# Six of seven sums of the heads' expert weights as three accumulating DMAs, with ten weight slots and new orders

## The chip, the cores and the metric

The kernel runs on one core of one Trainium2 chip. The metric is the device time of the whole program in microseconds (us). A core has five engines that run beside each other, each with its own instruction queue, in order: TensorE (PE), VectorE (DVE), ScalarE (ACT), GpSimd (POOL) and SyncE (SP), which here only issues DMAs.

## The reference

One layer of a perceiver-like model on x (64 batches x 64 rows x 128) and a context (64 x 128 x 96): cross attention with 16 heads, a tree attention with 16 heads, and a feed-forward part with product keys. The change lies in the last part:

```python
s1 = einsum('bshd,nd->bshn', q1, K1); s2 = einsum('bshd,nd->bshn', q2, K2)   # 8 heads, 32 keys each
v1, i1 = top_k(s1, 10);  v2, i2 = top_k(s2, 10)
vals, best = top_k(v1[..., :, None] + v2[..., None, :], 10)                 # 10 of the 1024 experts per head
scores = softmax(vals)
h = gelu(einsum('bsd,bshkd->bshk', x, W_down[expert_idx])) * scores
out = einsum('bshk,bshkd->bsd', h, W_up[expert_idx])
```

## The kernel before

The 4096 rows are 32 tiles of 128 rows (two batches a tile). No expert is gathered. For each head the kernel makes a dense row of 1024 weights: `e.s{h}` (PE) writes the 1024 sums of key scores to PSUM, `e.x{h}` (ACT) takes their exponent into `ew`, and `e.w{h}` (DVE, L1012) keeps those at or above the head's cut and writes zero elsewhere into a slot of `mw`, 128 x 1024 f32. POOL adds the eight heads' rows up into `wsum` in seven sums `e.a1` to `e.a7` (L1120). `e.wturn` (PE) transposes the sum, `e.gate` (DVE) multiplies it with the GELU of x times W_down (`e.hid` on PE, `e.gelu` on ACT with a table load before and after), `e.out` (PE) multiplies with W_up, and `e.add` (DVE) adds it to the residual `x3` and gives `y`, which `st.y` (SP) stores.

`mw` has NMW = 4 slots; head h uses slot h % 4. `e.w{h}` waits until the sum that read the slot is done.

The other steps that matter: `x.q0` to `x.q3` (PE, queries), copied out by `x.w0` to `x.w3`; `x.s0` to `x.s3` (PE, L377, scores, reading `cT`, which `ld.ct` loads); `x.x` (DVE, maxima), `x.e` (ACT, exponents, L705), `x.r` (DVE), `x.n` (POOL, L1071), `x.p` (PE, transposes), `x.t` (ACT), `y.m` (PE, mix with the context), `y.u` (ACT), `y.out` (PE, L439), `y.res` (DVE, L906, adds and takes statistics). Then the tree attention: `t.root` (POOL, L1058), `t.norm` (ACT, L686), `t.turn` (PE, L452), `t.sb`, `t.pv` (PE), `t.path` (DVE), `t.feat` (POOL), `t.fturn` (PE, L475), `t.fsb`, `t.sim`, `t.exp`, `t.mix`, `t.div`, `t.cturn`, `t.csb` (ACT, `actxT`), `t.out` (PE, L519), `t.res` (DVE). Then the keys: `k.root`, `k.norm`, `k.turn`, `k.high`, `k.low`, `k.key` (PE, L537 and L312 to L314, 512 columns), `k.top` (DVE), `k.split` (DVE), `k.kturn` (SP, a transposing DMA from `us` to `usT`, read by `e.s{h}`), `k.shift` (ACT, L766), `k.inner` (POOL), `k.cand` (DVE), `k.eb`, `k.z`, `k.lnz`.

The order on each engine is written out by hand in the five tables `PE_ORDER` to `SP_ORDER`: iteration i runs the steps from left to right, each for tile i minus its lag. Each step has its own semaphore; a step waits for its sources, for the readers of its destination, and for the step that last used its PSUM bank (table `BANK`).

Of the kernel before, what the change touches and what calls it, by code (L numbers as in the profile page):

```python
# [29 lines left out]
def build(nc, a):  # L30
# [3 lines left out]
    with ctx:  # L34
# [229 lines left out]
        def _(pe):  # L264
# [96 lines left out]
            def scores(k):  # L361
                def step(t):
                    if k == 0:
                        pe.wait_ge(s["x.w0"], t + 1)
                    elif k == 1:
                        pe.wait_ge(s["x.w3"], t + 1)
                    elif k == 2:
                        pe.wait_ge(s["x.w1"], t + 1)
                    elif k == 3:
                        pe.wait_ge(s["x.e0"], t + 1)  # L370
# [29 lines left out]
            def mix(k):  # L400
                def step(t):
                    if k == 0:
                        pe.wait_ge(s["x.t0"], t + 1)
                    elif k == 1:
                        pe.wait_ge(s["x.t1"], t + 1)
                    elif k == 2:
                        pe.wait_ge(s["x.t2"], t + 1)
# [36 lines left out]
            def t_turn(t):  # L444
                after(pe, "k.shift", t - 1)
# [5 lines left out]
                pe.wait_ge(s["t.norm"], t + 1)  # L451
                done("t.turn", pe.transpose(bank[BANK["t.turn"]][:, 0:128], xn2[:, t % 2, :], ident[:]))  # L452
            steps["t.turn"] = t_turn

            def paths_values(t):
                pe.wait_ge(s["t.sb"], t + 1)
# [84 lines left out]
            def hidden(t):  # L541
                after(pe, "e.w6", t - 1)
                at_ends(pe, "e.w6", t - 2)
                at_ends(pe, "e.w6", t - 3)
                at_ends(pe, "e.w6", t - 4)
                at_ends(pe, "e.w6", t - 5)
                at_ends(pe, "e.w6", t - 6)
# [495 lines left out]
        def _(pool):  # L1043
# [68 lines left out]
            def add_weights(h):  # L1112
                def step(t):
                    if h == 1:
                        pool.wait_ge(s["e.w0"], t + 1)
                        after(pool, "e.wturn", t - 2)
                    else:
                        pool.wait_ge(s[f"e.a{h - 1}"], t + 1)
                    pool.wait_ge(s[f"e.w{h}"], t + 1)
                    done(f"e.a{h}", pool.tensor_tensor(wsum[:, t % 2, :],  # L1120
                                                       mw[:, 0, :] if h == 1 else wsum[:, t % 2, :],
                                                       mw[:, h % NMW, :], ALU.add))
# [91 lines left out]
```

## Time and profile before

| | |
|---|---|
| runs of before | 1117.99 and 1122.17 us, median 1120.08 us |
| profiled execution | 1122.6 us, its span 1119.4 us |
| busy in the span | PE 984.9, DVE 889.4, ACT 907.5, POOL 829.9 us |
| share of the span | PE 88%, DVE 79%, ACT 81%, POOL 74% |
| granted TensorE clock, mean | 0.951 |
| DMA | 27.27 MB, mean 24 GB/s |

The profile is of one execution. Times are us from the start of the span. Busy shares are means over filling, steady part and drain; a wait is put down to the work that ended last before it.

### The profile page before, as it was taken

The page shows a single profiled execution, that of the slowest core. Times are in us where ns is not written, and L with a number is a line of the kernel's source. Part 1 is how long each engine was busy: PE and PEld are TensorE (multiplying, and loading weights), DVE is VectorE, ACT ScalarE, POOL GpSimd, SP SyncE. Part 2 cuts the span into 40 slices and gives each one's busy share as a digit, 9 for nine tenths or more (in the row PEclk, how much of TensorE's full clock was granted, in tenths as well). Part 3 has the DMA queues.
Part 4 walks back from the last instruction along what each step waited for, and adds up shares of the span by engine and source line. Part 5 has one row for each costly group of instructions (what it writes and reads, how often), then busy time and mean ns, then how long its engine had stood idle before and what let it go on. Part 6 is the DMA issues. An engine that isn't in the chain of part 4 may idle for free. (4 is left out here: it accounts for less than half of the span.)

```text
span 1119.4 us, 36025 instructions
## 1 busy us (share of the span) xinstructions
PE 984.9 (88%) x12440; PEld 793.3 (71%) x12440; DVE 889.4 (79%) x2941; ACT 907.5 (81%) x2223; POOL 829.9 (74%) x871
## 2 busy tenths in 40 slices
PE   6788998999988899999889999998998999899765
PEld 5666777777876777777677777776777777677533
DVE  3378788888888888888888888888888888888763
ACT  3668988888898888889888888988888889888652
POOL 1328777778877777888777787877787887777755
PEclk9989999999999999999999999999999999999765
DMA  6000000111010101111010110101011100010000
GB/s 163 13 22 20 19 16 22 25 25 26 20 23 15 25 22 26 25 20 26 11 26 22 25 25 23 23 12 25 22 25 25 26 20 23 14 21 19 13 13 5
DMA packets 70369, 27.27 MB, mean 24 GB/s; under 512 B 47312, under 2 KB 69936, under 8 KB 70192
## 3 DMA queue, kind: packets, MB, share of 16 engines
q1 hardware_dynamic: 69152, 24.58, 10.1%
q8 instruction: 103, 1.69, 0.6%
q14 instruction: 74, 0.61, 0.2%
q10 hardware_dynamic: 1040, 0.39, 0.1%
HBM read 14.47 MB, written 2.10 MB: 15 GB/s over the span
## 5 line engine op out<-in xcount | busy, mean ns | idle before, releaser
L1120 POOL TENSOR_TENSOR wsum<-wsum,mw 128x1024 f32<-128x1024 f32 x192 | 452.8, 2358 | 5.6
L1012 DVE SCALAR_TENSOR_TENSOR mw<-psF,cut,ew 128x1024 f32<-128x1024 f32 x256 | 326.4, 1276 | 49.8 <-ACT ew L795 49.7
L795 ACT ACTIVATE ew<-psF,lnz 128x1024 f32<-128x1024 f32 x256 | 283.6, 1120 | 15.0 <-PE psF L589 11.5
L589 PE MATMUL psF<-sel,usT 128*128 128x512 f16 x512 | 167.0, 411 | 33.0 <-DVE mw L1012 18.7
L1071 POOL TENSOR_TENSOR p<-p,rrow 128x512 f32<-128x512 f32 x128 | 133.1, 1040 | 74.5 <-DVE rrow L894 68.3
L705 ACT ACTIVATE p<-psXT,negmax 128x128 f32<-128x128 f32 x512 | 181.0, 377 | 3.2 <-DVE negmax L885 1.9
L377 PE MATMUL psXT<-cT,q 96*128 96x128 f32 x1024 | 144.5, 286 | 38.1 <-DMA cT<-cT_dram 31.8
L377 PEld LDWEIGHTS psXT<-cT,q 96*128 96x128 f32 x1024 | 132.7, 199 | 52.3 <-DVE q L626 41.8
L705 ACT ACTIVATION_READ_ACCUMULATOR p<-psXT,negmax 128x1 f32 x512 | 111.7, 218 | 0.0
L418 PE MATMUL psXT<-pT,c 128*32 128x384 f32 x768 | 98.7, 500 | 1.6 <-ACT pT L622 1.6
L885 DVE TENSOR_REDUCE negmax<-psXT 128x4 f32<-128x512 f32 x128 | 85.8, 670 | 16.4 <-PE psXT L377 16.4
L420 PE MATMUL psXT<-pT,c 128*32 128x128 f32 x768 | 97.3, 277 | 0.0
L312 PE MATMUL psXT<-xnT,qk 128*96 128x128 f16 x512 | 92.9, 223 | 1.8 <-DVE xnT L876 1.8
L1120 POOL TENSOR_TENSOR wsum<-mw 128x1024 f32<-128x1024 f32 x32 | 75.4, 2357 | 24.2 <-DVE mw L1012 24.2
L313 PE MATMUL psXT<-xnT,qk 128*96 128x128 f16 x512 | 92.9, 222 | 0.0
L314 PE MATMUL psXT<-xnT,qk 128*96 128x128 f16 x512 | 92.9, 222 | 0.0
L439 PE MATMUL psXT<-vo,uT 128*128 128x128 f32 x768 | 92.6, 278 | 0.0
L1058 POOL TENSOR_TENSOR rstd<-mv,halfneg 128x1 f32<-128x1 f32 x96 | 52.7, 549 | 53.7 <-DVE mv L862 53.7
L589 PEld LDWEIGHTS psF<-sel,usT 128*128 128x128 f16 x512 | 41.8, 101 | 66.1 <-DVE mw L1012 29.7
L439 PEld LDWEIGHTS psXT<-vo,uT 128*128 128x128 f32 x768 | 88.3, 192 | 0.0
L396 PE MATMUL psXT<-ident,p 128*128 128x128 f32 x512 | 79.9, 280 | 0.0
L420 PEld LDWEIGHTS psXT<-pT,c 128*32 128x32 f32 x768 | 79.7, 111 | 0.3
(134 smaller groups left out, 2372.5 us busy)
## 6 DMA issues: line engine op xcount, KB each, us to landing
cT<-cT_dram SPq DMA_DIRECT2D x32, 96.0 KB, 2.0
c<-c_dram SPq DMA_DIRECT2D x32, 96.0 KB, 2.0
x<-x_dram SPq DMA_DIRECT2D x32, 64.0 KB, 2.2
xr<-x_dram SPq DMA_DIRECT2D x32, 64.0 KB, 1.9
y_dram<-y SPq DMA_DIRECT2D x32, 64.0 KB, 1.5
wqT<-wqT_dram SPq DMA_DIRECT2D x1, 512.0 KB, 5.0
wo<-wo_dram SPq DMA_DIRECT2D x1, 512.0 KB, 6.3
wdT<-wdT_dram SPq DMA_DIRECT2D x1, 512.0 KB, 3.6
```

What stands on the lines that cost most here:

```text
L312: pe.matmul(out, left[:, 0, :], right[:, 0, :], start=not open_group, stop=False)
L313: pe.matmul(out, left[:, 0, :], right[:, 1, :], start=False, stop=False)
L377: mm = pe.matmul(bank[BANK[f"x.s{k}"]][:, i * M:i * M + M], q[:, b, h:h + 2, :].rearrange("c h q -> c (h q)"), cT[:, t % 2, b, :], start=T ...
L418: pe.matmul(to[32 * j:32 * j + 32], cols, probs[:, :, 0:3, :], start=True, stop=True, tile_position=(0, 32 * j))
L420: mm = pe.matmul(to[96:128, :, j, :], cols, probs[:, :, 3, :], start=True, stop=True, tile_position=(0, 96))
L439: mm = pe.matmul(out, uT[:, i, :, :].rearrange("c b q -> c (b q)"), vo[:, i, :], start=False, stop=(i == XH3 - 1))
L589: mm = pe.matmul(bank[BANK[f"e.s{h}"]][:, j * 512:j * 512 + 512], usT[:, t % 4, h, :], sel[:, j * 512:j * 512 + 512], start=True, stop=True)
L705: ins = act.activation(p[:, k, i, :], bank[BANK[f"x.s{k}"]][:, i * M:i * M + M], ACT.Exp, bias=negmax[:, k, i:i + 1], accum_out=rowsum[:, ...
L795: done(f"e.x{h}", act.activation(ew[:, h % NEW, :], bank[BANK[f"e.s{h}"]], ACT.Exp, bias=lnz[:, t % 4, h:h + 1]))
L1012: done(f"e.w{h}", dve.scalar_tensor_tensor(out=mw[:, h % NMW, :], in0=bank[BANK[f"e.s{h}"]], scalar=cut[:, t % 4, h:h + 1], in1=ew[:, h % ...
L1071: done(f"x.n{k}", pool.tensor_tensor(p[:, k, :, :], p[:, k, :, :], rrow[:, k, :].unsqueeze(2).to_broadcast([128, 4, M]), ALU.mult))
L1120: done(f"e.a{h}", pool.tensor_tensor(wsum[:, t % 2, :], mw[:, 0, :] if h == 1 else wsum[:, t % 2, :], mw[:, h % NMW, :], ALU.add))
```

## The change

`mw` gets ten slots, and head h of tile t uses slot (8t + h) % 10, so that heads 0 and 1, 2 and 3, and so on always lie side by side. Three DMAs that POOL issues add pairs of slots onto the pair of heads 0 and 1: `e.sa` the heads 2 and 3, `e.sb` 4 and 5, `e.sc` 6 and 7, each 128 x 2048 f32, each issued when the one before has landed. One POOL sum, `e.fin`, adds the two accumulator slots into `wsum`. `e.wturn` waits for `e.fin`. All five orders, the PSUM banks and the waits that follow from them are new.

```diff
-NEW, NMW = 4, 4
+NEW, NMW = 4, 10
+SUMS = ("e.sa", "e.sb", "e.sc")
...
+        def slot(t, h):
+            return (FH * t + h) % NMW
...
                     dve.wait_ge(s[f"e.x{h}"], t + 1)
-                    if h < NMW:
-                        after(dve, f"e.a{h + FH - NMW}", t - 1)
+                    if h < 2:
+                        after(dve, "e.sc", t - 2)
+                    elif h < 4:
+                        after(dve, "e.fin", t - 1)
                     else:
-                        dve.wait_ge(s[f"e.a{max(h - NMW, 1)}"], t + 1)
...
-            def add_weights(h):
...
+            def add_pairs(name, h, before):
+                def step(t):
+                    for i in range(h if before else 0, h + 2):
+                        pool.wait_ge(s[f"e.w{i}"], t + 1)
+                    if before:
+                        pool.wait_ge(s[before], 16 * (t + 1))
+                    pool.nop(nofuse=True)
+                    to, by = slot(t, 0), slot(t, h)
+                    pool.dma_start(mw[:, to:to + 2, :], mw[:, by:by + 2, :], accum_op=ALU.add).then_inc(s[name], 16)
+                return step
+            steps["e.sa"] = add_pairs("e.sa", 2, None)
+            steps["e.sb"] = add_pairs("e.sb", 4, "e.sa")
+            steps["e.sc"] = add_pairs("e.sc", 6, "e.sb")
+            def add_last(t):
+                pool.wait_ge(s["e.sc"], 16 * (t + 1))
+                after(pool, "e.wturn", t - 2)
+                done("e.fin", pool.tensor_tensor(wsum[:, t % 2, :], mw[:, slot(t, 0), :], mw[:, slot(t, 1), :], ALU.add))
...
 PE_ORDER = {
-    "e.s2": 5, "e.s1": 5, "x.q3": 3, "x.s1": 3, "e.s0": 5, "t.fturn": 4, "e.s3": 5, "x.s3": 3, "t.sim": 4,
-    "e.s4": 5, "e.wturn": 6, "t.mix": 4, "x.p0": 3, "e.s5": 5, "t.cturn": 4, "x.p2": 3, "t.out": 4, "x.p1": 3,
-    "e.s6": 5, "y.m0": 3, "y.m2": 3, "y.m1": 3, "k.turn": 4, "e.s7": 5, "x.p3": 3, "k.key": 4, "y.m3": 3,
-    "x.turn": 2, "e.hid": 4, "y.out": 3, "x.q0": 2, "x.q1": 2, "e.out": 6, "x.q2": 2, "t.turn": 3, "x.s2": 2,
-    "t.pv": 3, "x.s0": 2,
+    "e.s1": 5, "x.s1": 3, "e.s0": 5, "t.fturn": 4, "x.s3": 3, "e.s3": 5, "t.sim": 4, "e.wturn": 6, "e.s4": 5,
+    "t.mix": 4, "x.p0": 3, "e.s6": 5, "t.cturn": 4, "x.p2": 3, "x.p1": 3, "e.s5": 5, "t.out": 4, "y.m2": 3,
+    "x.p3": 3, "y.m0": 3, "y.m1": 3, "e.s7": 5, "k.turn": 4, "y.m3": 3, "k.key": 4, "x.turn": 2, "e.hid": 4,
+    "y.out": 3, "x.q0": 2, "x.q1": 2, "x.q2": 2, "t.turn": 3, "x.s0": 2, "e.s2": 4, "t.pv": 3, "x.q3": 2,
+    "x.s2": 2, "e.out": 6,
 }
 ACT_ORDER = {
-    "t.pexp": 4, "x.e2": 3, "k.lnz": 5, "e.x2": 5, "e.x1": 5, "x.e0": 3, "e.x0": 5, "t.fsb": 4, "e.x3": 5,
-    "x.e1": 3, "t.exp": 4, "e.x4": 5, "x.e3": 3, "x.t0": 3, "t.csb": 4, "e.x5": 5, "x.t2": 3, "x.t1": 3, "e.x6":
-    5, "k.norm": 4, "y.u2": 3, "k.high": 4, "y.u0": 3, "y.u1": 3, "x.t3": 3, "x.norm": 2, "e.x7": 5, "y.u3": 3,
-    "x.high": 2, "e.gelu": 4, "k.shift": 4, "x.w0": 2, "x.w1": 2, "t.norm": 3, "x.w2": 2, "t.sb": 3, "k.eb": 4,
-    "t.v": 3,
+    "e.x2": 5, "x.e2": 3, "e.x1": 5, "e.x0": 5, "t.fsb": 4, "e.x3": 5, "x.e1": 3, "t.exp": 4, "e.x4": 5, "x.e3":
+    3, "x.t0": 3, "t.csb": 4, "x.t2": 3, "x.t1": 3, "e.x5": 5, "y.u2": 3, "e.x6": 5, "k.norm": 4, "x.t3": 3,
+    "k.high": 4, "e.x7": 5, "y.u1": 3, "y.u0": 3, "y.u3": 3, "x.high": 2, "e.gelu": 4, "k.shift": 4, "x.w0": 2,
+    "x.norm": 1, "x.w1": 2, "t.norm": 3, "x.w2": 2, "t.sb": 3, "t.v": 3, "t.pexp": 3, "k.eb": 4, "x.e0": 2,
+    "k.lnz": 4,
 }
 DVE_ORDER = {
-    "e.add": 7, "k.z": 5, "t.path": 4, "x.x0": 3, "x.w3": 3, "e.w2": 5, "x.r2": 3, "e.w1": 5, "x.x1": 3, "x.r0":
-    3, "e.w0": 5, "e.w3": 5, "x.x3": 3, "x.r1": 3, "e.gate": 6, "t.div": 4, "e.w4": 5, "x.r3": 3, "t.res": 4,
-    "e.w5": 5, "x.stats": 1, "k.low": 4, "e.w6": 5, "k.top": 4, "k.split": 4, "x.low": 2, "e.w7": 5, "y.res": 3,
-    "k.cand": 4, "x.x2": 2,
+    "x.x2": 3, "e.add": 7, "e.w2": 5, "x.x1": 3, "e.w1": 5, "e.w0": 5, "x.r0": 3, "x.x3": 3, "x.r2": 3, "e.w3":
+    5, "e.gate": 6, "x.r1": 3, "t.div": 4, "e.w4": 5, "x.r3": 3, "x.stats": 1, "t.res": 4, "e.w5": 5, "e.w6": 5,
+    "k.low": 4, "e.w7": 5, "k.top": 4, "x.low": 2, "k.split": 4, "y.res": 3, "k.cand": 4, "x.x0": 2, "k.z": 4,
+    "t.path": 3, "x.w3": 2,
 }
 POOL_ORDER = {
-    "e.a7": 6, "t.feat": 4, "x.n2": 3, "x.n0": 3, "e.a1": 5, "x.n1": 3, "e.a2": 5, "x.n3": 3, "k.root": 4,
-    "e.a3": 5, "e.a4": 5, "e.a5": 5, "k.inner": 4, "e.a6": 5, "t.root": 3, "x.root": 1,
+    "x.n0": 3, "x.n2": 3, "e.sa": 5, "x.n1": 3, "x.n3": 3, "k.root": 4, "e.sb": 5, "x.root": 1, "k.inner": 4,
+    "e.sc": 5, "t.root": 3, "e.fin": 5, "t.feat": 3,
 }
 SP_ORDER = {
-    "st.y": 7, "ld.ct": 2, "ld.c": 2, "k.kturn": 4, "ld.x": 0, "ld.xr": 2,
+    "ld.x": 0, "ld.c": 2, "st.y": 7, "ld.xr": 2, "k.kturn": 4, "ld.ct": 1,
 }
```

## Rows read from the trace of the kernel before

**Rows 1.** Timeline of the GELU alone, one row a stretch, count and first and last start.

```profile
L786 ACT ACTIVATE gh<-psF x5: 1023/1023/1025, 267.1 to 396.6; 128x1024 f32<-128x1024 f32 x5
...
L786 ACT ACTIVATE gh<-psF x5: 1023/1023/1024, 883.4 to 1013.4; 128x1024 f32<-128x1024 f32 x5
```

**Rows 2.** Windows: busy us of each engine in a steady stretch, granted clock, DMA share.

```profile
300.00:500.00 200.00, 182.29 (x2382) 149.11 (x2380) 169.23 (x571) 172.63 (x421) 160.64 (x171) 0.98 0.12 24
```

**Rows 3.** Waits of PE, 300 to 900 us: us in total, times, longest.

```profile
PE psXT L377 <- DMA cT<-cT_dram: 22.4, 19, 1.2
PE psXT L519 <- ACT actxT L751: 10.3, 18, 0.7
PE psF L589 <- DVE y L1030: 7.9, 19, 0.4
PE psF L589 <- DVE mw L1012: 6.7, 18, 0.4
PE psXT L483 <- ACT featT L737: 4.5, 13, 0.3
```

**Rows 4.** Groups of instructions: POOL's sums, busy us and mean ns.

```profile
L1120 POOL TENSOR_TENSOR wsum<-wsum,mw 128x1024 f32<-128x1024 f32 x192 | 452.8, 2358 | 5.6
```

**Rows 5.** DMA queues and issues: KB each, us from issue to landing.

```profile
q1 hardware_dynamic: 69152, 24.58, 10.1%
...
x<-x_dram SPq DMA_DIRECT2D x32, 64.0 KB, 2.2
...
wdT<-wdT_dram SPq DMA_DIRECT2D x1, 512.0 KB, 3.6
...
usT<-us SPq DMA_TRANSPOSE x32, 3.2
```

**Rows 6.** Timeline 519 to 535 us: `k.key`, `k.top` and the GELU's table load.

```profile
522.79 0.38 PE L314 MATMUL psXT<-fqk,xn3T 128*128 128x512 f16 x1
...
523.31 1.67 DVE L951 MAX8 top<-psXT 128x8 f32<-128x32 f32 x16
...
525.66 1.28 ACT L785 ACT_TABLE_LOAD   x1 [0.88 <-PE psF L314]
```

**Rows 7.** Timeline from 506 us: the scores, and weights 2, 3 and 5 on DVE.

```profile
506.25 1.13 PE L377 MATMUL psXT<-cT,q 96*128 96x128 f32 x8 [1.18 <-DMA cT<-cT_dram]
506.42 1.28 DVE L1012 SCALAR_TENSOR_TENSOR mw<-psF,cut,ew 128x1024 f32<-128x1024 f32 x1 [0.31 <-ACT ew L795]
...
511.79 1.28 DVE L1012 SCALAR_TENSOR_TENSOR mw<-psF,cut,ew 128x1024 f32<-128x1024 f32 x1 [0.69 <-ACT ew L795]
...
519.00 1.28 DVE L1012 SCALAR_TENSOR_TENSOR mw<-psF,cut,ew 128x1024 f32<-128x1024 f32 x1
```

**Rows 8.** Timeline 496 to 504 us: from `y.res` to `t.turn`.

```profile
496.25 0.28 DVE L906 TENSOR_TENSOR x<-xr,psXT 128x128 f32<-128x128 f32 x1
...
497.07 0.60 ACT L766 ACTIVATE cand<-psXT 128x512 f32<-128x512 f32 x1
...
497.31 2.00 PE L611 MATMUL psF<-wup,gT 128*128 128x128 f32 x16
497.57 1.07 ACT L622 ACTIVATE q<-psXT 96x512 f32<-96x512 f32 x2
...
498.47 0.55 POOL L1058 TENSOR_TENSOR rstd<-mv,halfneg 128x1 f32<-128x1 f32 x1
...
499.49 0.49 ACT L686 ACTIVATE xn<-x,rstd 128x128 f32<-128x128 f32 x1 [0.85 <-POOL rstd L1061]
...
500.13 0.30 PE L452 MATMUL psXT<-ident,xn 128*128 128x128 f32 x1
```

**Rows 9.** Timeline of the drain: the last tile's weights, sums and transposes.

```profile
1091.94 2.48 DVE L1012 SCALAR_TENSOR_TENSOR mw<-psF,cut,ew 128x1024 f32<-128x1024 f32 x2 [1.09 <-ACT ew L795]
...
1095.74 14.47 POOL L1120 TENSOR_TENSOR wsum<-wsum,mw 128x1024 f32<-128x1024 f32 x6
...
1110.36 1.94 PE L601 MATMUL psF<-ident,wsum 128*128 128x128 f32 x8 [1.70 <-POOL wsum L1120]
```

More of the change, by code:

```diff
@@ L341, in step @@
                         at_ends(pe, "t.div", t - 7)
+                    elif k == 1:
+                        pe.wait_ge(s["x.high"], t + 1)
+                        pe.wait_ge(s["x.low"], t + 1)
                     elif k == 2:
@@ L363, in step @@
                     if k == 0:
-                        pe.wait_ge(s["x.w0"], t + 1)
+                        pe.wait_ge(s["x.w1"], t + 1)
                     elif k == 1:
+                        pe.wait_ge(s["x.e0"], t + 1)
+                    elif k == 2:
+                        after(pe, "t.sb", t - 1)
+                        at_ends(pe, "x.w0", t)
+                    elif k == 3:
                         pe.wait_ge(s["x.w3"], t + 1)
[L367 to L370, printed above, removed]
                     pe.wait_ge(s["ld.ct"], 16 * (t + 1))
@@ L392, in step @@
                     elif k == 3:
-                        pe.wait_ge(s["y.u2"], t + 1)
+                        pe.wait_ge(s["x.t2"], t + 1)
                     pe.wait_ge(s[f"x.n{k}"], t + 1)
@@ L402, in step @@
                     if k == 0:
+                        pe.wait_ge(s["x.t1"], t + 1)
+                    elif k == 1:
+                        pe.wait_ge(s["y.u2"], t + 1)
+                    elif k == 2:
                         pe.wait_ge(s["x.t0"], t + 1)
[L404 to L407, printed above, removed]
                     elif k == 3:
@@ L444, in t_turn, with paths_values @@
             def t_turn(t):
+                after(pe, "x.w0", t + 1)
+                at_ends(pe, "y.u3", t)
+                pe.wait_ge(s["t.norm"], t + 1)
+                done("t.turn", pe.transpose(bank[BANK["t.turn"]][:, 0:128], xn2[:, t % 2, :], ident[:]))
+            steps["t.turn"] = t_turn
+            def paths_values(t):
                 after(pe, "k.shift", t - 1)
@@ L450, in t_turn @@
                 at_ends(pe, "k.shift", t - 6)
[L451 to L456, printed above, removed]
                 if t == 0:
@@ L469, in feat_turn @@
                 after(pe, "x.e2", t + 1)
-                at_ends(pe, "y.u3", t)
+                at_ends(pe, "t.sb", t)
                 pe.wait_ge(s["t.feat"], t + 1)
@@ L542, in hidden @@
                 after(pe, "e.w6", t - 1)
[L543 to L547, printed above, removed]
+                at_ends(pe, "e.gate", t - 2)
+                at_ends(pe, "e.gate", t - 3)
+                at_ends(pe, "e.gate", t - 4)
+                at_ends(pe, "e.gate", t - 5)
+                at_ends(pe, "e.gate", t - 6)
+                at_ends(pe, "e.gate", t - 7)
                 if t == 0:
@@ L575, in step @@
                     elif h == 4:
-                        pe.wait_ge(s["e.w0"], t + 1)
+                        pe.wait_ge(s["e.w3"], t + 1)
                     elif h == 5:
+                        pe.wait_ge(s["e.w4"], t + 1)
+                    elif h == 6:
                         after(pe, "e.gate", t - 1)
-                        at_ends(pe, "e.w3", t)
-                    elif h == 6:
-                        pe.wait_ge(s["e.w4"], t + 1)
+                        at_ends(pe, "e.w0", t)
                     elif h == 7:
@@ L596, in w_turn @@
             def w_turn(t):
-                after(pe, "e.w3", t + 1)
-                at_ends(pe, "e.add", t - 1)
-                pe.wait_ge(s[f"e.a{FH - 1}"], t + 1)
+                after(pe, "e.w0", t + 1)
+                at_ends(pe, "e.w6", t)
+                pe.wait_ge(s["e.fin"], t + 1)
                 for c in range(EC):
@@ L607, in experts_out @@
                 after(pe, "e.w7", t + 1)
-                at_ends(pe, "e.gate", t)
+                at_ends(pe, "e.add", t - 1)
                 pe.wait_ge(s["e.gate"], t + 1)
@@ L1007, in step @@
                     dve.wait_ge(s[f"e.x{h}"], t + 1)
-                    if h < NMW:
-                        after(dve, f"e.a{h + FH - NMW}", t - 1)
-                    else:
-                        dve.wait_ge(s[f"e.a{max(h - NMW, 1)}"], t + 1)
-                    done(f"e.w{h}", dve.scalar_tensor_tensor(out=mw[:, h % NMW, :], in0=bank[BANK[f"e.s{h}"]],
+                    if h < 2:
+                        after(dve, "e.sc", t - 2)
+                    elif h < 4:
+                        after(dve, "e.fin", t - 1)
+                    else:
+                        after(dve, "e.sa" if h < 6 else "e.sb", t - 1)
+                    done(f"e.w{h}", dve.scalar_tensor_tensor(out=mw[:, slot(t, h), :], in0=bank[BANK[f"e.s{h}"]],
                                                              scalar=cut[:, t % 4, h:h + 1], in1=ew[:, h % NEW, :],
@@ L1110, in _ @@
             steps["t.feat"] = features
-            def add_weights(h):
+            def add_pairs(name, h, before):
                 def step(t):
[L1114 to L1122, printed above, removed]
-                return step
@@ L1124, in _ @@
-            for h in range(1, FH):
-                steps[f"e.a{h}"] = add_weights(h)
+                    for i in range(h if before else 0, h + 2):
[5 more added lines that the diff above has]
+                    pool.dma_start(mw[:, to:to + 2, :], mw[:, by:by + 2, :], accum_op=ALU.add).then_inc(s[name], 16)
@@ L1127, in _ @@
+                return step
+            steps["e.sa"] = add_pairs("e.sa", 2, None)
[5 more added lines that the diff above has]
+                done("e.fin", pool.tensor_tensor(wsum[:, t % 2, :], mw[:, slot(t, 0), :], mw[:, slot(t, 1), :], ALU.add))
+            steps["e.fin"] = add_last
             run(steps, POOL_ORDER)
@@ L1157 @@
 }
 BANK = {
[5 rows of a table removed]
[5 rows of a table added]
 }
-PE_VO = "x.s2"
+PE_VO = "x.s0"
 PE_KEYS = "x.p0"
-ACT_VO = "x.e2"
+ACT_VO = "x.e0"
 ACT_KEYS = "x.t0"
-DVE_BIAS = "x.x2"
+DVE_BIAS = "x.x0"
 DVE_KEYS = "t.div"
```

5 lines of the change are left out of this document (1 added, 4 removed), and 10 rows, old and new, of the table BANK.

## Prediction, made before the change was run

> **What bounds the kernel now.** I read the busy shares first, then the period of the steady part, then PE's waits in it, then one period in order of time, and last the drain. In the steady part the period is the distance between two GELUs: from 267.1 to 1013.4 us there are 23 periods [rows 1], so 746.3 / 23 = 32.45 us a tile. In the window 300 to 500 us PE is busy 182.3 us of 200 us at a granted clock of 0.98 (the 2.4 GHz level), so 29.6 us of a period and 2.9 us of gaps; DVE is busy 27.5 us, ACT 28.0 us and POOL 26.1 us of each period [rows 2]. PE is the fullest engine, and the others are full enough that its gaps come from orders and latencies. The gaps of PE by releaser between 300 and 900 us, 18.5 periods, are: 22.4 us at the scores for `cT` (1.2 us a tile), 10.3 us for `actxT` (0.55), 7.9 us for `y` (0.43), 6.7 us for `mw` (0.36), 4.5 us for `featT` (0.24) [rows 3]: 2.8 us a tile, the whole gap. No row there names a POOL sum. So the first thing to see is that freeing POOL gives nothing by itself; what can give is the new order on PE, and what can take is any new wait in PE's queue.
>
> **POOL's sums.** A sum takes 2358 ns [rows 4]. Six a tile go: 6 x 2.36 = 14.2 us off POOL's 26.1 us. One, `e.fin`, stays. POOL then has about 12 us of work and three DMA issues. No POOL-issued DMA is in this trace; even 1.5 us each leaves POOL half idle. On the critical path in the steady part this is worth 0.
>
> **The price T of one accumulating DMA**, from its issue to its semaphore. It moves two slots, 128 x 2048 f32, 1 MiB in and 1 MiB of destination changed. The trace of before has none. Nearest rows: 64 KB of `x` land in 2.2 us and 512 KB of `wdT` in 3.6 us [rows 5], so 1.4 us for 448 KB, 3.2 us for a MiB, and a fixed part of 2.0 us. If the data passes once, T is 5.2 us; if destination and source are both read, one after the other, 8.4 us. I take the middle, 6.8 us, and keep both ends. These DMAs are a chain: sb waits for sa, sc for sb, `e.fin` for sc.
>
> The Trainium skill, "Collectives: The Full Stack", section "Why ReduceScatter is half of AllGather", says that an adding DMA reads two sources and so halves the rate, and "DMA: Bandwidth & Descriptors", section "Anatomy of one DMA", gives 2.0 us fixed and 436 GB/s for a DMA that GpSimd issues. An estimate from these pages is 2.0 + 2 x 2.4 = 6.8 us, the chain then being hidden; by the double pass of the rows it would not be. No row of before can decide.
>
> **Where the chain must fit.** I count from the end K of `k.key` on PE (matmuls at 522.79, end 523.17 us) [rows 6]. One period earlier K is 490.72. `e.w3` ends at 513.07, K - 10.1, and `e.w5` at 520.28, K - 2.9 [rows 7]. `y.m3` (0.8 us) now goes ahead of `k.key`, so K itself moves 0.8 later: w3 ends at K - 10.9, w5 at K - 3.7, and `e.w7`, no longer behind `k.split`, before `k.top`. So sa is issued at K - 10.8 and is back at K - 4.0, sb goes at K - 3.6 and is back at K + 3.2. On POOL sc stands behind `k.inner`, which needs `k.top` (1.67 us from 523.31 [rows 6] and a subtraction of 0.7: 2.4 us after K) and 1.1 us of its own: issue K + 3.9, back K + 10.7, `e.fin` ends K + 13.2. The first that needs it is `e.w2` of the next tile (slots 2 and 3 are the accumulator of the tile before), on DVE behind `e.add`: 506.42 us in the row, K + 15.7 [rows 7]. Slack 2.5 us. If all three DMAs are slow the limit is -10.8 + 3T + 2.5 = 15.7, T = 8.0 us. Behind e.sb on POOL wait `x.root` and `k.inner`, behind e.sc `t.root`, behind e.fin `t.feat`; at T = 6.8 us none of them is late (`t.root` needs `y.res`, K + 5.5; `t.feat` needs `t.path`, about K + 13.7, and its reader `t.fturn` stands at K + 18). At 5.2 us nothing changes; at 8.4 us the period grows by 3 x 0.4 = 1.2 us. The two extra needs of ten slots (`e.w0` and `e.w1` on sc two tiles back, `e.w4` to `e.w7` on sa and sb of the tile before) are met a good half period early.
>
> **PE's order, what goes.** (a) `ld.ct` moves from lag 2, behind `st.y`, to lag 1 behind `k.kturn`, and is issued almost a period before `x.s0` reads it; and `x.q3` no longer stands directly ahead of `x.s1`, but has `x.s2`, `e.out` (2.00 us) and `e.s1` between them, which covers `x.w3`. The 1.2 us wait at 506.25 us [rows 7] goes. (b) `t.out` gets `x.p1` and `e.s5` more in front: the 0.55 us for `actxT` goes. (c) `e.s0` now has `e.s1` and `x.s1` after the start of `e.w2`: 0.3 of the 0.36 us for `mw` goes. Sum 2.05 us a tile. Left: `y` and `featT`, 0.7 us.
>
> **What comes.** `e.out` used to lie between `x.q1` and `x.q2` and covered the way from `y.out` to `t.turn`: add and statistics from 496.25 us, `t.root`, `t.norm` at 499.49, `t.turn` at 500.13 [rows 8]. Now only three products lie there. PE: `x.turn`, `e.hid`, `y.out` end at K + 4.5, three products of 0.7 us at K + 6.6. By `y.res` (end K + 5.5), root 1.1 and norm 0.6 us `t.turn` could start at K + 7.35: a gap of 0.75. But ACT is the later one: table load at 525.66 us was K + 2.5 [rows 6], now K + 1.9; in the row `k.shift` follows 3.86 us later (497.07 against 525.66 - 32.45), so K + 5.75; then `k.shift` 0.6, `x.w0` 0.54, `x.norm` 0.5 (new ahead of it), `x.w1` 0.54, `t.norm` 0.5: `t.turn` at K + 8.45, a gap of 1.85 us. I take 1.85 and keep 0.75 as the other end. `k.kturn` now stands on SP behind `ld.xr`, which waits for `y.res`: issue K + 6.0, landing 3.2 us later [rows 5], K + 9.2, and `e.s2`, now at lag 4 and so its reader in the same period, is reached at K + 9.85. Cost 0, the gap at `t.turn` covers it; without that cover 0.4 us. `ld.c` now leads `st.y` on SP and waits for `y.m0`; `st.y` moves to mid-period, and its slot is used again two tiles later: 0. `e.out` is now directly ahead of `e.s1` in the same bank, so PE waits for `e.add` (0.28 us and two semaphores), about what the `y` gap is now: 0.
>
> Sum a tile: -2.05 + 1.85 = -0.2 us, times 31 = -6 us.
>
> **The drain.** The last four first weights end at 1094.4 us, POOL's seven sums at 1110.2 us, and `e.wturn` follows at 1110.36 [rows 9]. With the DMAs: 1094.4 + 0.2 + 3 x 6.8 + 2.4 + waits 0.2 = 1117.6, 7.4 us later; with `e.w2` some 0.6 us later, +8 us. At T = 5.2 us it is +3, at 8.4 us +13. The filling I take as unchanged, +-3 us.
>
> **Total.** The profiled execution took 1122.6 us around a span of 1119.4 us; the median of the runs is 1120.1, 2.5 less. 1122.6 - 6 + 8 - 2.5 = 1122 us.
>
> **Rivals.** (1) Better packing. If ACT reaches `t.norm` early, because the tables are loaded sooner when PE has no wait for `cT`, only the 0.75 us gap stays: -1.3 us a tile, -40 us, and 1088 us. For it: ACT is busy only 28.0 us of a period [rows 2]; against: the chain of table loads starts with `e.hid`, which PE's own order fixes. Chance 0.28. (2) The chain of DMAs becomes the loop. Place: `e.w2` on DVE behind `e.fin`. It decides from T = 8.0 us, and costs 3 us a tile for each us more. At 8.4 us: 1.2 x 31 = 37 us, and 5 more in the drain: 1164 us; at 9 us 1220. For it: the double pass in the rows; against: the slack of 2.5 us at 6.8. Chance 0.20. (3) sc and the transposing DMA meet. sc runs from K + 3.9 to K + 10.7, `k.kturn` from K + 6.0. The queue of SP's DMAs takes 10.1% of 16 engines [rows 5], 3.3 us a period, so each could stretch the other by up to that; `usT` at K + 12.4 instead of 9.2 would hold `e.s2` for 2.5 us: +78 us, 1200 us; half of it, 1.0 us, 1153 us. Chance 0.12. By the skill's DMA page, section "Issuing engines are not separate DMA queues", the DMAs of all queues share the same engines and interleave, which speaks for this rival; in before the queues never met, so no row bears it out.
>
> **Chances.** Forecast (within 2%, which is about what a measurement of this kernel can tell from no change) 0.40, its own range 1098 to 1142 us; rival 1 0.28, faster by over 2%; rivals 2 and 3 together 0.32, slower by over 2%. The range that holds 8 in 10 reaches from 1085 us into rival 1 to 1175 us into rivals 2 and 3.
>
> **What would show it.** Distance of two GELUs 32.2 us. PE's waits without `cT` and `actxT`, and with a new line at L452, `t.turn` for `xn`, of about 60 us in all. POOL busy about 40%. DVE's `mw` rows waiting for `wsum` or a DMA mean rival 2; PE's L589 waiting for the DMA of `usT` means rival 3. A `t.turn` wait under 1 us a tile means rival 1. The prediction fails in its first step if T lies outside 5.2 to 8.4 us.

## The result, and the profile after

The kernel after took 1296.37 us (1292.35 and 1300.38) against 1120.08 us; the ratio is 1.158, 95% interval 1.150 to 1.166. The forecast was 1122 us, within a range of 1085 to 1175 us. Times here are medians of the executions within 1.5% of the fastest of their kernel. The profiled execution took 1292.35 us around a span of 1290.2 us.

From the page of the profile of the kernel after: the busy row, the granted clock in 40 slices, the two DMA queues that count, the chain that ended last by engine, and the issues of the new DMAs (count, KB, median us to landing).

```profile
PE 1033.5 (80%) x12440; PEld 844.1 (65%) x12440; DVE 888.2 (69%) x2941; ACT 914.6 (71%) x2223; POOL 474.2 (37%) x775
...
PEclk9988999888989888889989888999888899989865
...
q0 software_dynamic: 13824, 100.67, 39.2%
q1 hardware_dynamic: 69152, 24.58, 8.3%
...
DMA 38%; PE 25%; issue 12%; ACT 10%; DVE 8%; POOL 6%; POOLq 1%; SPq 0%; DVEq 0%; ACTq 0%
...
mw<-mw POOLq DMA_DIRECT2D x96, 1024.0 KB, 7.6
```

POOL is relieved as foreseen, from 830 us busy to 474. PE is still the fullest engine, at 80%. Of the chain that ended last, 38% is DMA. (In before the profile follows that chain back over some 7% of the span alone, so the two shares can't be compared.)

Where the time is: GELU to GELU, the 31 periods ran from 78.3 to 1236.6 us, 37.37 us each, against 71.7 to 1078.4 us, 32.47 us each, in before (over its steady part 32.45 [rows 1]). That is 152 of the 171 us by which the spans differ. The filling is 6.6 us longer and the drain 12.6 us (53.6 against 41.0 us).

```profile
L794 ACT ACTIVATE gh<-psF x32: 1024/1024/1025, 78.3 to 1236.6; 128x1024 f32<-128x1024 f32 x32
```

PE's waits of the kernel after, 300 to 1100 us (us in total, times, longest), stand beside [rows 3]:

```profile
PE psXT L454 <- ACT xn L694: 73.7, 22, 4.9
PE psF L597 <- DMA usT<-us: 44.7, 11, 11.1
PE psXT L511 <- ACT am L752: 8.4, 21, 0.5
PE psF L597 <- DVE y L1041: 8.0, 21, 0.4
```

`cT` and `actxT` are gone, as predicted. In their place PE waits 3.4 us a tile for `t.norm`, and on some tiles up to 11.1 us for `usT`. To see who is behind `t.norm`, follow POOL's queue. This is POOL's timeline of the kernel after over one period (start, duration, and idle time before with its releaser); the L1132 rows are e.sa, e.sb, e.sc in turn, L1141 is e.fin:

```profile
627.90 0.91 POOL L1132 DMA_DIRECT2D mw<-mw  x1 [0.64 <-DVE mw L1023]
...
637.22 0.91 POOL L1132 DMA_DIRECT2D mw<-mw  x1 [2.80 <-DMA mw<-mw]
...
641.28 0.61 POOL L1100 TENSOR_TENSOR cand<-tops 128x32 f32<-128x32 f32 x3
646.36 0.92 POOL L1132 DMA_DIRECT2D mw<-mw  x1 [4.47 <-DMA mw<-mw]
647.01 0.87 POOL L1069 TENSOR_TENSOR rstd<-mv,halfneg 128x1 f32<-128x1 f32 x1
...
653.57 2.35 POOL L1141 TENSOR_TENSOR wsum<-mw 128x1024 f32<-128x1024 f32 x1 [5.25 <-DMA mw<-mw]
655.90 0.25 POOL L1111 TENSOR_SCALAR path<-path 128x80 f32<-128x80 f32 x1
...
664.73 0.91 POOL L1132 DMA_DIRECT2D mw<-mw  x1 [0.46 <-issue]
```

From sa to sb 9.3 us, sb to sc 9.1, sc to e.fin 7.2. The row at 647.01 is `t.root`, issued right behind sc. Its source was ready at 643.30 us, as DVE's timeline shows with the last row of `y.res`:

```profile
643.15 0.15 DVE L870 TENSOR_SCALAR mv<-mv 128x1 f32<-128x1 f32 x1
```

So `t.root` stood 3 us in POOL's queue behind sc's wait for the landing of sb. The chain that ended last says the same. Here it is over the same stretch (start, duration, what):

```profile
637.22 8.52 DMA mw<-mw
...
646.36 0.92 POOL mw L1132
647.28 0.62 POOL rstd L1069
...
648.36 0.50 ACT xn L694
...
649.00 0.45 PE psXT L454
649.44 1.83 PE psXT L383 x8
...
655.30 1.80 PE psF L619 x16
...
657.12 0.30 DVE y L1041
...
659.61 1.01 DVE mw L1023
...
662.24 1.91 POOL p L1082 x2
...
664.73 8.84 DMA mw<-mw
```

A loop is closed: sa, sb, sc, `t.root`, `t.norm`, `t.turn`, PE's list to `x.s1`, DVE's to `x.r0`, then `x.n0` and `x.n2` on POOL, and sa again, 36.8 us. The score matmuls behind the gap take 1.83 us for what `x.s2` does in 0.95 us later in the same period: in the window 649.0 to 651.5 us the granted clock was 0.50, the 1.2 GHz level, after PE had waited 4.76 us.

### The profile page after: what moved, and what is told of

The parts are those of the page before. It is cut to its first block, busy times and chain, and to the rows that moved or that the text cites. A ratio compares the mean times of both kernels' runs of the same rounds, so it can differ in the third digit from the quotient of the medians.

```text
span 1290.2 us, 35924 instructions
## 1 busy us (share of the span) xinstructions
PE 1033.5 (80%) x12440; PEld 844.1 (65%) x12440; DVE 888.2 (69%) x2941; ACT 914.6 (71%) x2223; POOL 474.2 (37%) x775
## 4 chain that ended last, share of the span: by engine, by line
DMA 38%; PE 25%; issue 12%; ACT 10%; DVE 8%; POOL 6%; POOLq 1%; SPq 0%; DVEq 0%; ACTq 0%
DMA mw<-mw 30%; PE psXT L383 8%; DMA usT<-us 7%; PE psF L597 4%; PE psF L619 4%; DVE mw L1023 3%; ACT p L713 3%; ACT ew L803 3%; POOL p L1082 2%; ACT pT L630 1%; PE psXT L482 1%; DVE top L959 1%; POOL feat L1115 1%; POOL mw L1132 1%; ACT xn L694 1%
## 5 line engine op out<-in xcount | busy, mean ns | idle before, releaser
L803 ACT ACTIVATE ew<-psF,lnz 128x1024 f32<-128x1024 f32 x256 | 286.5, 1121 | 39.4 <-PE psF L597 34.5
L383 PE MATMUL psXT<-cT,q 96*128 96x128 f32 x1024 | 170.5, 320 | 1.2 <-DVE q L634 1.2
L1132 POOL DMA_DIRECT2D mw<-mw x96 | 87.2, 908 | 217.7 <-DMA mw<-mw 184.4
L383 PEld LDWEIGHTS psXT<-cT,q 96*128 96x128 f32 x1024 | 156.3, 230 | 9.5 <-ACT p L713 1.8
L1141 POOL TENSOR_TENSOR wsum<-mw 128x1024 f32<-128x1024 f32 x32 | 75.1, 2348 | 190.7 <-DMA mw<-mw 190.7
L736 ACT ACTIVATE v<-psXT 128x128 f32<-128x128 f32 x32 | 8.9, 278 | 150.3 <-PE psXT L471 150.3
L424 PE MATMUL psXT<-pT,c 128*32 128x384 f32 x768 | 104.2, 496 | 9.2 <-ACT pT L630 6.8
L317 PE MATMUL psXT<-xnT,qk 128*96 128x128 f16 x512 | 106.5, 242 | 1.8 <-DVE xnT L884 1.8
L318 PE MATMUL psXT<-xnT,qk 128*96 128x128 f16 x512 | 105.5, 240 | 0.0
L319 PE MATMUL psXT<-xnT,qk 128*96 128x128 f16 x512 | 105.3, 239 | 0.0
L426 PE MATMUL psXT<-pT,c 128*32 128x128 f32 x768 | 102.3, 277 | 0.0
L454 PE MATMUL psXT<-ident,xn 128*128 128x128 f32 x32 | 11.5, 360 | 109.3 <-ACT xn L694 109.3
L694 ACT ACTIVATE xn<-x,rstd 128x128 f32<-128x128 f32 x96 | 47.9, 498 | 66.9 <-POOL rstd L1072 66.8
L1069 POOL TENSOR_TENSOR rstd<-mv,halfneg 128x1 f32<-128x1 f32 x96 | 71.4, 744 | 55.7 <-DVE mv L870 55.7
```

The source lines that it names most:

```text
L317: pe.matmul(out, left[:, 0, :], right[:, 0, :], start=not open_group, stop=False)
L318: pe.matmul(out, left[:, 0, :], right[:, 1, :], start=False, stop=False)
L319: return pe.matmul(out, left[:, 1, :], right[:, 0, :], start=False, stop=True)
L383: mm = pe.matmul(bank[BANK[f"x.s{k}"]][:, i * M:i * M + M], q[:, b, h:h + 2, :].rearrange("c h q -> c (h q)"), cT[:, t % 2, b, :], start=T ...
L424: pe.matmul(to[32 * j:32 * j + 32], cols, probs[:, :, 0:3, :], start=True, stop=True, tile_position=(0, 32 * j))
L426: mm = pe.matmul(to[96:128, :, j, :], cols, probs[:, :, 3, :], start=True, stop=True, tile_position=(0, 96))
```

## The experiments

Theory Q says that this loop through POOL's queue sets the period; theory F, the loop through the slots (`e.fin` frees the slots of `e.w2`; [rows 7] were my measure for it); theory O, the new orders. Periods below are GELU to GELU over all 31, and like the waits they are of the one profiled execution of a kernel.

**e1: the three DMAs out.**

```diff
-                    pool.dma_start(mw[:, to:to + 2, :], mw[:, by:by + 2, :], accum_op=ALU.add).then_inc(s[name], 16)
+                    pool.memset(mark[:], 0.0).then_inc(s[name], 1)
```

> The kernel after, with each of the three accumulating DMAs replaced by a one-column memset on POOL, so that heads 2 to 7 are left out of the sum; all orders, slots and waits stay. Theory Q (the loop runs through POOL's queue: sa, sb, sc, and t.root behind e.sc) and theory F (the loop runs through e.fin and e.w2) both expect the period to fall from 37.8 us to that of the orders alone, 32.3 us by the prediction's count, and about 1120 us. Theory O (the new orders themselves cost the time) expects it to stay above 1200 us.

Measured: 1117.33 us, ratio 0.997 (0.996 to 0.999), period 32.52 us. O is out: without the DMAs the new orders run as fast as before.

**e2: the new orders with POOL's seven sums**, in place of the DMAs:

```diff
+    "x.n0": 3, "x.n2": 3, "e.a1": 5, "x.n1": 3, "e.a2": 5, "x.n3": 3, "k.root": 4, "e.a3": 5, "e.a4": 5,
+    "x.root": 1, "e.a5": 5, "k.inner": 4, "t.root": 3, "e.a6": 5, "e.a7": 5, "t.feat": 3,
```

> The kernel after with its orders, banks and ten slots, but the seven sums done by POOL as in before (e.a1 to e.a7 in the places that POOL's queue has for them). Q and F: 1115 to 1140 us, since only the DMAs cost. O: above 1200 us. Against e1 it shows whether freeing POOL is worth anything: the prediction said 0 in the steady part and some microseconds in the drain.

Measured: 1171.06 us, ratio 1.045 (1.043 to 1.047). A miss by 31 us: between 300 and 900 us PE now waits 18.8 us for `x.n` on POOL. In these orders POOL's relief is worth 54 us (e2 against e1), which the prediction had at nothing in the steady part; 3 of the 54 us are in the drain.

**e3: `t.root` ahead of `e.sc`.**

```diff
-    "e.sc": 5, "t.root": 3, "e.fin": 5, "t.feat": 3,
+    "t.root": 3, "e.sc": 5, "e.fin": 5, "t.feat": 3,
```

> The kernel after with one step moved: t.root ahead of e.sc in POOL's order. Q: t.root runs when y.res is done, some 3 us earlier, and PE's wait for xn at t.turn (3.5 us a tile) falls under 2 us; the chain sa, sb, sc, e.fin, e.w2 is next late, so the period falls from 37.8 to about 34 us and the time to 1170 to 1210 us. F: nothing behind e.sc matters, the time stays within 1% of 1296 us.

Measured: 1299.44 us, period 38.14 us (of an execution of 1308.66 us), against theory Q alone. PE's wait for `xn` fell to 1.3 us a tile as Q said, but the time did not: DVE now waits 51.0 us (14 times between 300 and 900 us) for `wsum` at `e.w2`. Something as long stood right behind.

**e4: copies in place of additions.**

```diff
-                    pool.dma_start(mw[:, to:to + 2, :], mw[:, by:by + 2, :], accum_op=ALU.add).then_inc(s[name], 16)
+                    pool.dma_start(mw[:, to:to + 2, :], mw[:, by:by + 2, :]).then_inc(s[name], 16)
```

> The kernel after with plain copies in place of the accumulating DMAs (same slots, same 1 MiB, issued by POOL), so the sum is not computed. If the second read of an accumulation doubles the data time, the landing falls from 7.1 us undisturbed to about 4.7 us and the time to under 1180 us by both Q and F. If the packets or POOL's descriptors set it, the landing stays near 7 us and the time near 1290 us.

Measured: 1193.62 us (one execution), 14 us over the most that was expected, with the landing as expected.

**e5: additions of half the size.**

```diff
-                    pool.dma_start(mw[:, to:to + 2, :], mw[:, by:by + 2, :], accum_op=ALU.add).then_inc(s[name], 16)
+                    pool.dma_start(mw[:, to:to + 1, :], mw[:, by:by + 1, :], accum_op=ALU.add).then_inc(s[name], 16)
```

> The kernel after with each accumulating DMA halved to one slot (128 x 1024 f32, 512 KB), so heads 3, 5 and 7 are left out of the sum. If the data time goes with the bytes, the landing falls from 7.0 to about 4.6 us, as for the copies of 1 MiB, whose DMA engine time was half, and the time comes out near theirs, 1170 to 1200 us. If the fixed part rules, the landing stays over 6 us and the time over 1250 us.

Measured: 1183.56 us (one execution), as expected. Their DMA rows, first e4 and then e5 (packets, MB, share of 16 engines; KB and median us to landing):

```profile
q0 software_dynamic: 13824, 100.67, 22.2%
...
mw<-mw POOLq DMA_DIRECT2D x96, 1024.0 KB, 5.0
```

```profile
q0 software_dynamic: 13824, 50.34, 22.3%
...
mw<-mw POOLq DMA_DIRECT2D x96, 512.0 KB, 4.7
```

The engines' time for one DMA is the share times the span by 96: 0.392 x 1290.2 / 96 = 5.27 us in the kernel after, 2.76 us for the copy, 2.74 us for half an addition. An addition costs the DMA engines 1.9 times a copy of its size, and the least landing between 300 and 900 (after: 1100) us was 6.9, 4.5 and 4.4 us. The trace so agrees with the Trainium skill, "Collectives: The Full Stack", section "Why ReduceScatter is half of AllGather": the add reads two sources. The prediction's estimate from the Trainium skill, 6.8 us, lies 0.1 us under that least landing. It is the price of a DMA alone: the four additions of the kernel after beside which no other queue moved a packet landed in 6.8 to 7.0 us.

**e6: both tree steps ahead of the waits.**

```diff
-    "e.sc": 5, "t.root": 3, "e.fin": 5, "t.feat": 3,
+    "t.root": 3, "e.sc": 5, "t.feat": 3, "e.fin": 5,
```

> The kernel after with t.root ahead of e.sc and t.feat ahead of e.fin in POOL's order, so that neither tree step stands behind a wait for a DMA. Theory Q2 (two queue loops of nearly equal length: t.root behind e.sc, t.feat behind e.fin) expects both gone and only the slot loop left, three DMAs at 9.1, 9.1 and 7.8 us, e.fin 2.4 us and some 7 to 8 us from e.w2 to e.w3: a period of 35.5 to 36.5 us, 1215 to 1250 us. Theory F (the slot loop w2, w3, sa, sb, sc, fin alone sets the time, t.feat does not matter) expects 1296 us within 1.5%.

Measured: 1291.65 us, period 37.57 us, as theory F said (the other execution took 1316.15 us). POOL's timeline of e6, one period of sa, sb, sc, e.fin and sa:

```profile
617.08 0.89 POOL L1132 DMA_DIRECT2D mw<-mw  x1 [1.63 <-DVE mw L1023]
...
626.67 0.91 POOL L1132 DMA_DIRECT2D mw<-mw  x1 [3.07 <-DMA mw<-mw]
...
635.23 0.91 POOL L1132 DMA_DIRECT2D mw<-mw  x1 [1.71 <-DMA mw<-mw]
...
643.30 2.34 POOL L1141 TENSOR_TENSOR wsum<-mw 128x1024 f32<-128x1024 f32 x1
...
654.65 0.89 POOL L1132 DMA_DIRECT2D mw<-mw  x1 [1.63 <-DVE mw L1023]
```

and DVE's of e6, `e.w2` and `e.w3` of the next tile:

```profile
645.75 1.28 DVE L1023 SCALAR_TENSOR_TENSOR mw<-psF,cut,ew 128x1024 f32<-128x1024 f32 x1 [2.57 <-POOL wsum L1141]
...
652.70 1.28 DVE L1023 SCALAR_TENSOR_TENSOR mw<-psF,cut,ew 128x1024 f32<-128x1024 f32 x1 [0.81 <-ACT ew L803]
```

9.6 + 8.6 + 8.1 us of DMAs, 2.3 of `e.fin`, 0.1 to the start of `e.w2` and 8.9 from there to sa: 37.6 us. Nothing of the tree stands between. This is a second loop, as long as the first.

**e7: two DMAs instead of three**, heads 6 and 7 by POOL, and `t.root` ahead of the wait for sb:

```diff
-    "e.sc": 5, "t.root": 3, "e.fin": 5, "t.feat": 3,
+    "e.p7": 5, "t.root": 3, "e.p0": 5, "e.fin": 5, "t.feat": 3,
```

> The kernel after with e.sc taken out: POOL adds heads 6 and 7 into wsum (2.4 us while sb is in flight), then the two accumulator slots (two more sums behind sb), and t.root stands ahead of those two. The chain after e.w3 is then 2 x 9.2 + 4.8 us instead of 9.2 + 9.1 + 7.7 + 2.4 us, 5 us shorter. If the chain's length sets the time, the period falls to about 33 us and the time to 1125 to 1160 us. If the meeting of the transposing DMA with the accumulating ones is the main cost, it stays over 1200 us.

Measured: 1160.49 us, ratio 1.033 (1.028 to 1.039), period 33.59 us (of an execution of 1167.34 us), at the upper end of what the chain's length gives. Two things changed at once here, the chain and the place of `t.root`, so e7 does not tell them apart.

**e8: the kernel before with `ld.ct` early.**

```diff
-    "st.y": 7, "ld.ct": 2, "ld.c": 2, "k.kturn": 4, "ld.x": 0, "ld.xr": 2,
+    "st.y": 7, "ld.c": 2, "k.kturn": 4, "ld.x": 0, "ld.xr": 2, "ld.ct": 1,
```

> The kernel before with ld.ct alone moved, from lag 2 behind st.y to lag 1 at the end of SP's order. The prediction booked PE's 1.2 us wait for cT as removed by two edits together. If the load alone ended it, the period falls 1.2 us and the time to 1083 us (-3.3%). If x.w3 on DVE, which ended 0.1 us before in the row, is as late, the time stays within 0.5% of 1120 us.

Measured: 1120.51 us, ratio 1.000 (0.997 to 1.003). The 22.4 us that [rows 3] put down to `cT` are there again, now put down to `q`, which `x.w3` writes. `ld.ct` alone gives nothing. From PE's waits of e8, 300 to 900 us:

```profile
PE psXT L377 <- DVE q L626: 22.4, 19, 1.2
```

**e9 and e10: other seats in the ten slots**, e9 on e6, e10 on the kernel after:

```diff
-            return (FH * t + h) % NMW
+            return (FH * t + SEAT[h]) % NMW
+SEAT = {2: 0, 1: 1, 0: 4, 3: 5, 4: 6, 5: 7, 6: 2, 7: 3}
...
+                    if SEAT[h] < 2:
+                        after(dve, "e.sb", t - 2)
+                    elif SEAT[h] < 4:
+                        after(dve, "e.fin", t - 1)
+                    else:
+                        after(dve, "e.sc" if SEAT[h] < 6 else "e.sa", t - 1)
```

> The kernel of e6 (t.root ahead of e.sc, t.feat ahead of e.fin) with the heads seated otherwise in the ten slots: heads 2 and 1, the first made, are the accumulator pair; 0 and 3, then 4 and 5, then 6 and 7 are added by sa, sb, sc. The accumulator's slots then go to heads 6 and 7 of the next tile, the last made, and heads 0 and 3 take the slots that sc has read. Theory F (the slot loop e.w2, e.w3, sa, sb, sc, e.fin of 37.5 us sets e6): the loop is now sc landed, e.w0 to e.w3, sa, sb, sc, without e.fin, e.w2 and e.w1, 26.2 + 5.4 = 31.6 us, so it stops binding; the period falls to 33 to 34.5 us and the time to 1130 to 1190 us. If the DMAs' own time (meeting SP's DMAs) sets the time, it stays over 1270 us.

> The kernel after with the new seats alone, POOL's order as it is (t.root behind e.sc, t.feat behind e.fin). The slot loop is gone, the queue loop through t.root is left: 9.2 + 9.1 us to the issue of sc and 18.4 us from there over t.root, t.turn, PE's list and x.n0, x.n2 back to sa, 36.8 us. Theory Q expects 36 to 37.8 us a tile and 1250 to 1300 us. If only the slot loop mattered in the kernel after, it falls with e9 to under 1200 us.

Measured: e9 1146.60 us, ratio 1.021 (1.013 to 1.029); e10 1303.56 us. With the kernel after and e6 that is a table of two by two:

| | tree steps behind the waits | tree steps ahead |
|---|---|---|
| heads 2, 3 in the accumulator's old slots | 1296 (after) | 1292 (e6) |
| heads 6, 7 in them | 1304 (e10) | 1147 (e9) |

Either loop alone holds the kernel near 1300 us; some 150 us come back only with both cut. Neither Q nor F was right alone. The profiled execution of e9 is its longest, 1163.31 us.

**e11: `k.kturn` ahead of `ld.xr` on SP, on e9.**

```diff
-    "ld.x": 0, "ld.c": 2, "st.y": 7, "ld.xr": 2, "k.kturn": 4, "ld.ct": 1,
+    "ld.x": 0, "ld.c": 2, "st.y": 7, "k.kturn": 4, "ld.xr": 2, "ld.ct": 1,
```

> The kernel of e9 with k.kturn ahead of ld.xr in SP's order, so that the transposing DMA goes out when k.split is done, over 1.5 us before e.sc, which stands behind t.root and y.res on POOL. In the traces usT lands in 3.0 to 3.3 us when it goes out well apart from an accumulating DMA's issue, and in 8 to 16 us when it goes out within 0.8 us behind one. If these meetings are what keeps e9 (one period of 43.5, one of 39.2 and one of 36.4 us among periods of 31.5 to 33.3) above e1, the long periods go, the mean period falls from 33.5 to about 32.4 us, and the time to 1115 to 1128 us. If the meetings only move (usT then meets sb), it stays at 1140 to 1165 us.

Measured: 1103.95 us, ratio 0.986 (0.984 to 0.989): 1.4% faster than before, and 11 us faster than the least that was expected. PE's waits of e11, 300 to 900 us:

```profile
PE psXT L455 <- ACT xn L695: 24.6, 19, 1.4
PE psF L598 <- DVE y L1042: 7.5, 19, 0.4
PE psXT L512 <- ACT am L753: 6.2, 19, 0.3
...
PE psF L598 <- DMA usT<-us: 0.2, 1, 0.2
```

Its window over the same stretch (busy us of PE, PEld, DVE, ACT, POOL, granted clock, DMA share):

```profile
300.00:900.00 600.00, 551.72 (x7349) 449.56 (x7348) 516.62 (x1735) 533.42 (x1314) 279.74 (x456) 1.00 0.62 123
```

**e12: `x.norm` behind `t.sb` on ACT, on e11.**

```diff
-    "x.norm": 1, "x.w1": 2, "t.norm": 3, "x.w2": 2, "t.sb": 3, "t.v": 3,
+    "x.w1": 2, "t.norm": 3, "x.w2": 2, "t.sb": 3, "x.norm": 1, "t.v": 3,
```

> The kernel of e11 with x.norm moved behind t.sb in ACT's order. The prediction found 0.5 us of PE's gap at t.turn in x.norm standing ahead of t.norm. If ACT's list sets that gap (1.3 us in e1 and e9), it falls by 0.5 us a tile, 15 us in all against e11, more if the clock then no longer falls to 1.2 GHz behind the gap (a period with such a fall is 1.65 us longer in e1). If t.root sets it, nothing changes against e11.

Measured: 1105.42 us, no gain on e11, where 15 us were expected. PE's wait for `xn` fell from 24.6 to 17.4 us in that stretch, so `x.norm` did stand in the way, but the one for `y` rose from 7.5 to 11.3 us and that for `usT` from 0.2 to 2.1: most was given back within the period.

**e13, e14 and e15: the same SP edit alone**, on the kernel after, on e2 and on e1.

> The kernel after with k.kturn ahead of ld.xr alone; seats and POOL's order as they are. If the meetings of usT with the accumulating DMAs (2.1 us a tile of PE's waits in the trace of after) come on top of the two loops, the time falls by about 60 us to 1230 us. If the loops alone set the period (36.8 us in an undisturbed stretch), it falls to 1260 to 1280 us at most.

> The kernel of e2 (the new orders, the seven sums on POOL) with k.kturn ahead of ld.xr. If the small wait for usT (0.43 us a tile) is what it saves, as in e11, the time falls from 1171 to 1125 to 1160 us. Above e11's 1104 us means that the DMAs are worth something in these orders; as fast as e11 means that the orders alone made e11's gain.

> The kernel of e1 (the new orders, no sums of heads 2 to 7) with k.kturn ahead of ld.xr. If e11 hides its three DMAs entirely in the steady part, this runs at the same period, 31.5 us, and differs only by the drain, some 8 to 12 us: 1092 to 1097 us. If e11 still pays for them, this is below 1085 us.

Measured: e13 1236.0 us (ratio 1.104), 60 us of the 176 back, and PE's waits for `usT`, 44.7 us in the kernel after between 300 and 1100 us, are gone from its trace. The meetings of the two kinds of DMA are in these 60 us, but how much of them is theirs alone is not shown: the same edit gives 24 us where no DMA adds (e1 to e15) and 15 us with the sums on POOL (e2 to e14). e14 1156.49 us, 1.033 (1.030 to 1.035); e15 1093.55 us, 0.977 (0.974 to 0.981). e15's period is 31.62 us (70.8 to 1051.0) and e11's 31.59 us (70.8 to 1050.1): in e11 the DMAs are free in the steady part, and cost 12.7 us in the drain (50.9 against 38.2 us). The sums on POOL cost 63 us in nearly the same orders (e14 against e15), and e14 is slower than before. So in these orders the gain of e11 comes only with the DMAs that make room on POOL. Whether it needs the new orders too was not tried.

## Why the prediction was wrong

1. **The price T.** Taken 6.8 us, range 5.2 to 8.4. The least landing was 6.9 us between 300 and 1100 us, and 6.8 to 7.0 with no other queue's packets beside it, so the middle was right for a DMA alone. But the step "sa is issued at K - 10.8 and is back at K - 4.0, sb goes at K - 3.6" took a link of the chain for such a landing. Two parts came on top. With packets of other queues beside them sa took 8.7 and sb 8.5 us to land in the period shown, sc 7.1 (medians over the kernel after: 8.3, 7.7 and 7.4 us), and from the landing to the issue of sb or sc there are 0.6 us. The links of that period were 9.3, 9.1 and 7.2 us instead of 6.8. The range's upper end, 8.4 us, was below the first two.

2. **"At T = 6.8 us none of them is late."** This step failed hardest. I named `t.root` behind e.sc and checked it at the middle value alone; at my own upper end, 8.4 us, sc would have gone out at K + 6.0, already behind `y.res` at K + 5.5. At the measured links sc goes out at K + 8.5 (646.36, with K at 637.88 us), 3 us after `y.res`, and `t.root`, `t.norm`, `t.turn` and all of PE's list move with it; and the loop closes through `x.n2` and sa. It was no rival in the list.

3. **"Slack 2.5 us ... the limit is T = 8.0 us."** Rival 2 was the right mechanism with too small a price. With e6's mean link of 8.75 us it gives 32.3 + 3 x 0.75 = 34.5 us; measured 37.57. The missing 3 us lie between `e.w2` and sa: 8.9 us, where the count from K implied 5.8, in three parts. 0.8 us is a mistake in the count: `e.w3` was counted from the K that `y.m3` moves, `e.w2` from the old one. From `e.w2`'s start to `e.w3`'s end is 6.65 us in [rows 7], so the slack was 1.7 us and the limit T = 7.7 us. 1.6 us more come since behind a late `e.w2` the rows of heads 1, 0 and 3 follow 1.8, 1.8 and 3.4 us apart, `e.w3` waiting for its exponent. The last 0.6 us lie between `e.w3`'s end and the issue of sa, which I had at 0.1.

4. **Rival 3, the meeting of sc and `k.kturn`**, was real: half of it was priced 31 us, the whole 78, and e13 gives at most 60. That the size fits is partly luck. I had each stretch the other by up to 3.3 us in every period; measured were 2 us for `usT` in four of the 32 tiles, 5 us in eight and 12 us in one. It came on top of the loops, not in their place.

5. **PE's order.** Removed 2.05 and added 1.85 us a tile, net -0.2: e1 has 32.52 against 32.47 us, right as a sum, but by parts that cancel. Of (a), e8 shows that `ld.ct` alone would have given nothing; in before too the weight load of that product, at 506.23 us, waits 1.30 us for `q`. In e1 `t.turn`'s gap is 1.3 us, not 1.85 (24.9 us in 19 times), and `k.kturn` behind `ld.xr`, booked at 0, costs 0.43 us (8.1 us in 19 times). That small one matters most: see the last section. (K + 5.5 + 1.1 + 0.6 is K + 7.2, not 7.35, so the gap of rival 1 was 0.6.)

6. **"On the critical path this is worth 0"** was read from the old order and never tested in it. In the new one POOL's sums cost 54 us (e2 against e1) and 63 us (e14 against e15).

7. **The drain**: forecast +8 us, measured +12.6, as at my upper end of T. The filling, taken as unchanged within 3 us, took 6.6 us more in the profiled execution. That is hardly the change's: to the first GELU there are 78.3 us in the kernel after and 78.2 in e7, but 71.5 in e1, 71.9 in e3 and 71.7 in e6, against 71.7 in before.

What makes additions land late is not tried by a run, but the traces point at one thing: packets of 16 KB in the queue q8, which the profile calls instruction. In the kernel after such a packet started 0.6 to 5.9 us behind the issue of `e.sa` in all 19 tiles in which it landed in 8.1 to 8.8 us, and in none of the other 13, in which it took 6.8 to 7.7 us. `e.sb` landed in 8.3 to 8.8 us in 14 tiles, all with such a packet 1.3 to 6.5 us behind its issue, and in 6.9 to 7.9 us in the other 18, two of which had one at 6.4 or 6.5 us. Two additions of the drain, with nothing of SP's in flight, from the issue at 1187.64 us and from the one at 1223.29 us:

```profile
q0 software_dynamic: 144, 1.05, 58.2%
q8 instruction: 1, 0.02, 0.7%
...
mw<-mw POOLq DMA_DIRECT2D x1, 1024.0 KB, 8.8
```

```profile
q0 software_dynamic: 144, 1.05, 73.7%
...
mw<-mw POOLq DMA_DIRECT2D x1, 1024.0 KB, 7.0
```

What stays open: how one such packet can cost more than 1 us, and whether the old orders with the DMAs would have held, which was not tried.

## What to carry to other kernels

A DMA that replaces engine work puts its landing into the queue of the engine that must wait for it: for each step behind such a wait, work out the loop that closes through it at the upper end of the price, and move the steps that don't need the data ahead. When undoing one suspect changes nothing, look for a second loop of the same length before dropping it; the table of two by two told what the single edits hid. Slots in a ring go to the heads that are made last, and a transfer that others wait for at once is put ahead of loads in its queue.
